# Attention in a Trainium2 decoder layer: keys and values in a phase of their own through DRAM, units of four heads by 256 rows

## The reference, cut to what matters

```
k = (K @ Wk.T + bk).reshape(n, lk, H, D)      # K = V = ctx, (32, 77, 256); H 16, D 64
v = (V @ Wv.T + bv).reshape(n, lk, H, D)
scores = jnp.einsum('nqhd,nkhd->nqkh', q, k) / jnp.sqrt(jnp.float32(D))
attn = jax.nn.softmax(scores, axis=2)
out = jnp.einsum('nqkh,nkhd->nqhd', attn, v)
out = out.reshape(n, lq, H * D)
return (out @ Wo.T + bo).reshape(n, lq, E)
```

## Time and profile before

| | us |
|---|---|
| median of 3 runs | 2664.46 |
| lowest and highest | 2661.05, 2668.21 |
| profiled execution | 2667.21 |
| its span, first to last instruction | 2665.4 |
| TensorE busy | 2418.4 (91%) |
| VectorE busy | 1942.1 (73%) |
| ScalarE busy | 1349.4 (51%) |
| GpSimd busy | 1274.9 (48%) |

### The profile page before, as it was taken

One profiled execution on the slowest core, in us unless ns is written; L12 is line 12 of the kernel. 1 busy time (PEld: TensorE's weight loads), 2 busy tenths in 40 slices (PEclk: granted clock), 3 DMA queues, 4 the chain that ended last, 5 costly groups with the idle time before them and its releaser, 6 DMA issues. The chain is left out here.

```text
span 2665.4 us, 60791 instructions
## 1 busy us (share of the span) xinstructions
PE 2418.4 (91%) x18124; PEld 2197.3 (82%) x18125; DVE 1942.1 (73%) x5342; ACT 1349.4 (51%) x2881; POOL 1274.9 (48%) x1444
## 2 busy tenths in 40 slices
PE   7999999999968999999999999999992999999866
PEld 5777777777757999999999999999992899999833
DVE  7988888888854666666666666666672778877768
ACT  5555565655544544444444444444441566665523
POOL 4676667676642222233222332223321677876656
PEclk9999999999979999999999999999996999999955
DMA  3011111111011111211111111111107677776578
GB/s 133 29 36 35 31 30 32 35 35 35 28 38 63 56 49 55 67 66 53 57 54 66 66 48 63 54 66 66 45 33 287 227 242 252 246 253 221 185 246 272
DMA packets 170802, 263.44 MB, mean 99 GB/s; under 512 B 33560, under 2 KB 123296, under 8 KB 170720
## 3 DMA queue, kind: packets, MB, share of 16 engines
q1 hardware_dynamic: 156672, 225.70, 26.1%
q0 software_dynamic: 12960, 35.67, 3.7%
q10 hardware_dynamic: 1088, 1.07, 0.1%
HBM read 180.79 MB, written 81.59 MB: 98 GB/s over the span
## 5 line engine op out<-in xcount | busy, mean ns | idle before, releaser
L1290 ACT ACTIVATE b_qT<-b_ps_qk,b_bq_c 128x256 f32<-128x256 f32 x256 | 121.6, 475 | 397.8 <-PE b_ps_qk L1134 397.8
L1371 DVE TENSOR_REDUCE b_mx<-b_ps_s 128x4 f32<-128x308 f32 x256 | 121.6, 475 | 204.9 <-PE b_ps_s L1167 110.1
L1189 PE MATMUL b_ps_o<-b_vv,b_pT 77*128 77x65 f32 x2048 | 259.5, 269 | 0.8 <-DVE b_o_n L1391 0.8
L1189 PEld LDWEIGHTS b_ps_o<-b_vv,b_pT 77*128 77x128 f32 x2048 | 248.7, 192 | 6.2 <-issue 5.4
L570 DVE SCALAR_TENSOR_TENSOR a_conv<-a_xc_pad,a_cw,a_conv 128x256 f32<-128x256 f32 x384 | 236.1, 674 | 9.4 <-ACT a_conv L457 9.4
L1301 ACT ACTIVATE b_pe_<-b_sd 128x308 f32<-128x308 f32 x256 | 118.0, 461 | 217.9 <-DVE b_sd L1375 215.1
L1589 POOL TENSOR_TENSOR b_ve<-b_mv,b_ln_eps 128x1 f32<-128x1 f32 x64 | 12.2, 191 | 412.9 <-DVE b_mv L1414 412.9
L1977 POOL DMA_INDIRECT made_scratch<-c_o_s,c_to x142 | 150.2, 1058 | 90.7 <-issue 48.5
L112 PE MATMUL c_ps_h<-c_xT_hi,c_w 128*128 128x256 f32 x568 | 169.0, 298 | 23.6 <-DMA c_b_c<-in_c_b 14.6
L1167 PE MATMUL b_ps_s<-b_kz,b_qT 128*128 128x154 f32 x1024 | 188.3, 306 | 0.0
L112 PE MATMUL c_ps_o<-c_w,c_h_hi 128*128 x568 | 161.4, 284 | 20.1 <-DMA c_w<-parts_scratch 16.5
(11 more groups left out here) (266 smaller groups left out, 8563.7 us busy)
## 6 DMA issues: line engine op xcount, KB each, us to landing
c_w<-parts_scratch SPq DMA_DIRECT2D x79, 1024.0 KB, 16.3
c_xa<-sent_scratch SPq DMA_DIRECT2D x71, 260.0 KB, 2.7
parts_scratch<-b_w_cut SPq DMA_DIRECT2D x32, 512.0 KB, 4.6
d_got<-made_scratch SPq DMA_DIRECT2D x32, 512.0 KB, 5.4
a_xT_f<-in_xT SPq DMA_DIRECT2D x32, 256.0 KB, 3.1
a_x_f<-in_x SPq DMA_DIRECT2D x32, 256.0 KB, 2.6
x_scratch<-a_x_t SPq DMA_DIRECT2D x32, 256.0 KB, 2.2
b_xa<-x_scratch SPq DMA_DIRECT2D x32, 256.0 KB, 2.9
```

The source lines that it names most:

```text
L1189: last = pe.matmul(ps_o[:, (HD + 1) * i:(HD + 1) * i + HD + 1], pT[:, u.par, i, :], vv[:, b.par, G * g + i, :], start=True, stop=True)
L1290: act.activation(qT[:, b.par, m, :], ps_qk[:, 0:L], ACT.Identity, bias=bq_c[:, m:m + 1])
L1371: dve.tensor_reduce(mx[:, u.par, :], s, AX.X, ALU.max).then_inc(s_mx, 1)
```

## The change

The keys and the values of all sequences are computed ahead of the attention, in `keys_values_phase`, with float32r splits for both. It works on chunks of eight sequences: two groups of four sequences (308 wide) for the keys and five tiles of up to 128 context rows for the values, and writes both to DRAM (10.1 MB each). The cutting of the experts' 32 weight parts moves here too, with its loads (8.4 MB) and stores (16.8 MB). The working space lies in what will be `w2`.

In the attention a unit is four heads by all 256 rows, so a step has four turns. Keys and values come back from DRAM. The negated maximum is the bias of the exponential, which makes one instruction per 77 columns: eight in a unit. VectorE sums the exponentials and divides them before they are turned. `attend` has the values stationary, 64 columns for one head, and the turned probabilities moving, 256 wide; the even head of a pair goes to partitions 0 to 63 of the result and the odd one to 64 to 127. The result is already turned, so `turn_o` is gone. `ps_s`, which was two banks used in turn, is now one pair of banks that the next unit waits for. The experts' `w2` and rows are loaded in the attention's first eight steps (`load_later`).

```diff
-    PER = 8
+    PER = 4
...
+            def load_part(i):
+                if i >= 2:
+                    sp.wait_ge(s_cut_lo, i - 1)
+                sp.dma_start(w_raw[:, i % 2, :], routing.w_parts[i, :, :]).then_inc(s_raw[i % 2], 16)
+
+            def store_part(i):
+                sp.wait_ge(s_cut_lo, i + 1)
+                sp.dma_start(routing.parts[i, :, :],
+                             w_cut[:, i % 2, :, :].rearrange("p h n -> p (h n)").bitcast(F32)).then_inc(s_cut_out[i % 2], 16)
...
+            def store_keys(i):
+                sp.wait_ge(s_kc, MH * (i + 1))
+                sp.dma_start(keys[GROUP * i:GROUP * i + GROUP, :, :].rearrange("s p n -> p s n"),
+                             k_s[:, i % 2, :, :, :].rearrange("p s m k -> p s (m k)")).then_inc(s_k_out[i % 2], 16)
...
+            def store_values(ch, t):
+                i, (r, n) = ch * len(TILES) + t, TILES[t]
+                sp.wait_ge(s_vc, 2 * (i + 1))
+                sp.dma_start(values[ROWS * ch + r:ROWS * ch + r + n, :], v_s[0:n, i % 2, :]).then_inc(s_v_out[i % 2], 16)
...
+            for ch in range(CHUNKS):
+                for sub in range(SUBS):
+                    next_part()
+                    next_part()
+                    store_keys(ch * SUBS + sub)
+                if ch + 2 < CHUNKS:
+                    load_c(ch + 2)
+                for t in range(len(TILES)):
+                    next_part()
+                    store_values(ch, t)
...
+                for sub in range(SUBS):
+                    for m in range(MH):
...
+                        for k in range(KD):
+                            last = split3(pe, ps_k[i % 4][:, 0:N],
+                                          (wk_hi[:, k, P * m:P * m + P], wk_lo[:, k, P * m:P * m + P]),
+                                          (c_hi[:, par, k, N * sub:N * sub + N], c_lo[:, par, k, N * sub:N * sub + N]),
+                                          k == 0, k == KD - 1)
+                        last.then_inc(s_k, 1)
...
+                        for k in range(KD):
+                            last = split3(pe, ps_v[i % 4][0:n, :], (c_hi[:, par, k, r:r + n], c_lo[:, par, k, r:r + n]),
+                                          (wv_hi[:, k, 512 * half:512 * half + 512],
+                                           wv_lo[:, k, 512 * half:512 * half + 512]), k == 0, k == KD - 1)
+                        last.then_inc(s_v, 1)
...
+                    for m in range(MH):
+                        act.wait_ge(s_k, i * MH + m + 1)
+                        act.activation(k_s[:, i % 2, :, m, :], ps_k[(i * MH + m) % 4][:, 0:N].rearrange(
+                            "p (s k) -> p s k", s=GROUP), ACT.Identity, bias=weights.bk_c[:, m:m + 1]).then_inc(s_kc, 1)
...
+            for i in range(PARTS):
+                pool.wait_ge(s_raw[i % 2], 16 * (i // 2 + 1))
+                if i >= 2:
+                    pool.wait_ge(s_cut_out[i % 2], 16 * (i // 2))
+                pool.tensor_copy(w_cut[:, i % 2, 0, :], w_raw[:, i % 2, :]).then_inc(s_cut_hi, 1)
+                pool.wait_ge(s_cut_hi, i + 1)
+                pool.tensor_tensor(w_cut[:, i % 2, 1, :], w_raw[:, i % 2, :], w_cut[:, i % 2, 0, :].bitcast(F32),
+                                   ALU.subtract).then_inc(s_cut_lo, 1)
...
-        ps_s = [ctx.enter_context(nc.psum_tensor(f"b_ps_s{i}", [P, 512], F32)) for i in range(2)]
...
+        ps_s = ctx.enter_context(nc.psum_tensor("b_ps_s", [P, GM, 512], F32))
...
+            def load_keys(b):
+                if not b.before(2):
+                    sp.wait_ge(s_s, b.ago(2).count(4, 4))
+                for a in range(2):
+                    half = slice(HD * a, HD * a + HD)
+                    sp.dma_start(kz[half, b.par, a, :, :].rearrange("p m k -> p (m k)"),
+                                 keys[bass.ds(b.value(), 1), half, :].rearrange("o p n -> (o p) n")
+                                 ).then_inc(s_kz_in[b.par], 16)
+
+            def load_values(b):
+                if not b.before(2):
+                    sp.wait_ge(s_oT, b.ago(2).count(4, 4))
+                sp.dma_start(vv[:, b.par, :], values[bass.ds(b.value() * LK, LK), :]).then_inc(s_vv_in[b.par], 16)
...
+            def load_later(b):
+
+                if b.known() and b.value() < E:
+                    e = b.value()
+                    sp.dma_start(w2[:, e, :, :, :].rearrange("p q h n -> p q (h n)").bitcast(F32),
+                                 routing.parts[4 * e + 2:4 * e + 4, :, :].rearrange("q p n -> p q n")).then_inc(s_ahead, 16)
+                    sp.dma_start(weights.rows[:, e, :, :], rows_in[e, 0:2, :].partition_broadcast(P)).then_inc(s_ahead, 16)
...
-                for k in range(KD):
-                    split3(pe, ps_qk[:, 0:L], (wq_hi[:, k, P * m:P * m + P], wq_lo[:, k, P * m:P * m + P]),
-                           (xT_hi[:, b.par, k, :], xT_lo[:, b.par, k, :]), k == 0, k == KD - 1)
-                for k in range(KD):
-                    last = pe.matmul(ps_qk[:, L:L + LK], wk_f[:, k, P * m:P * m + P], c_f[:, b.par, k, :],
-                                     start=(k == 0), stop=(k == KD - 1))
-                last.then_inc(s_qk, 1)
...
+                    pe.wait_ge(s_qc, u.ago(1).count(1, 1))
+                for i in range(GM):
+                    at = slice(P * (GM * g + i), P * (GM * g + i) + P)
                     for k in range(KD):
-                        last = split3(pe, ps_x[0:LK, :], (c_hi[:, b.par, k, :], c_lo[:, b.par, k, :]),
-                                      (wv_hi[:, k, 512 * half:512 * half + 512],
-                                       wv_lo[:, k, 512 * half:512 * half + 512]), k == 0, k == KD - 1)
-                    last.then_inc(s_v, 1)
-                return run
+                        last = split3(pe, ps_q[:, L * i:L * i + L], (wq_hi[:, k, at], wq_lo[:, k, at]),
+                                      (xT_hi[:, b.par, k, :], xT_lo[:, b.par, k, :]), k == 0, k == KD - 1)
+                last.then_inc(s_q, 1)
...
+                pe.wait_ge(s_qc, u.count(1, 1))
+                if not u.before(1):
+                    pe.wait_ge(s_exp, u.ago(1).count(1, 1))
                 for i in range(GM):
-                    last = pe.matmul(ps_s[u.par][:, 2 * LK * i:2 * LK * i + 2 * LK],
-                                     qT[:, b.par, GM * g + i, P * j:P * j + P],
-                                     kz[:, b.par, GM * g + i, :, :].rearrange("p a k -> p (a k)"),
-                                     start=True, stop=True)
+                    for j in range(NT):
+                        last = pe.matmul(s_scores[:, i, 2 * j:2 * j + 2, :], qT[:, u.par, i, P * j:P * j + P],
+                                         kz[:, b.par, :, GM * g + i, :], start=True, stop=True)
...
+                for i in range(GM):
+                    for j in range(NT):
+                        for a in range(2):
+                            at = L * a + P * j
+                            last = pe.transpose(ps_pT[0:LK, i, at:at + P], pn[:, u.par, 4 * i + 2 * j + a, :], ident)
                 last.then_inc(s_pT, 1)
...
-                for i in range(G):
-                    last = pe.matmul(ps_o[:, (HD + 1) * i:(HD + 1) * i + HD + 1], pT[:, u.par, i, :],
-                                     vv[:, b.par, G * g + i, :], start=True, stop=True)
-                last.then_inc(s_o, 1)
...
                 for i in range(GM):
-                    last = pe.transpose(ps_oT[:, P * i:P * i + P], flat[:, P * i:P * i + P], ident)
+                    for a in range(2):
+                        at = HD * (G * g + 2 * i + a)
+                        last = pe.matmul(ps_oT[HD * a:HD * a + HD, L * i:L * i + L], vv[:, b.par, at:at + HD],
+                                         pT[:, u.par, i, L * a:L * a + L], start=True, stop=True)
                 last.then_inc(s_oT, 1)
...
+            def turn_x2(b):
+                pe.wait_ge(s_x2, b.count(NT, NT))
+                if over(b, 3):
+                    pe.wait_ge(s_base, b.ago(1).count(1, 1))
+                else:
+                    pe.wait_ge(s_xlo, b.ago(-3).count(1, 1))
+                if not b.before(1):
+                    pe.wait_ge(s_x2c, b.ago(1).count(1, 1))
+                for j in range(NT):
...
             run_steps(pe, n_seq, by_unit(
-                [(queries_keys, 0, 1), (scores, 0, 2), (turn_p, 1, 2), (attend, 2, 2), (turn_o, 3, 2), (project, 4, 2)],
-                {0: [(values(0), 1)], 1: [(turn_x2(0), 3)], 2: [(rank, 4)], 3: [(values(1), 1)], 4: [(gate(0), 3)],
-                 5: [(turn_x, 0)], 6: [(turn_x2(1), 3)], 7: [(gate(1), 3)]}), peel=8)
+                [(queries, 0, 1), (scores, 1, 1), (turn_p, 3, 1), (attend, 4, 1), (project, 5, 1)], {},
+                {0: [(rank, 4)], 1: [(turn_x, 0)], 2: [(turn_x2, 3)], 3: [(gate, 3)]}), peel=8)
...
+                for c in range(C):
+                    last = act.activation(pe_[:, u.par, c, :], s_scores[:, c // (C // GM), c % (C // GM), :], ACT.Exp,
```

(58 more changed lines are left out.)

631 lines of the change are left out of this document (292 added, 339 removed).

## The result

| | before | after |
|---|---|---|
| median of 4 runs, us | 2666.34 | 2473.47 |
| lowest and highest | 2661.05, 2670.03 | 2468.74, 2481.10 |
| profiled execution's span | 2665.4 | 2473.7 |
| TensorE busy | 2418.4 | 2201.1 |
| mean granted clock | 0.953 | 0.944 |

The changed kernel takes 0.928 of the time before (95% interval 0.925 to 0.931), 193 us less. The forecast was 2516, the range 2451 to 2635.

The account below looks back on a forecast made before the run. TensorE was taken to bound the attention. Against the profiled 2667.2 us, -297 for the attention, +168 for the new phase, -5 and -17 for small terms sum to -151, so 2516 us; range 2451 to 2635.

Parts of the forecast that it names:

- the sum: Whole kernel: attention -297, new phase +168, way to the first query -5, w2 loads -17, together -151 us.
- eight take the time of five: Attend: eight half-width records overlap only between neighbours on different halves, 1.19 us, taken as 1.3 with changes of width.
- the bound of fully abreast: Attend's lower bound: two heads of a pair run fully side by side on different column halves, 0.95 us.
- the change of width: Attend: going to half width and back on TensorE costs about 0.1 us a unit, 13 us in all.
- the rival of the drain: Attend: changing to half width and back empties TensorE, 41 us in place of 13, 2544 us; chance 0.08.
- The new phase: Keys and values ahead of the attention: SyncE's queue sets it, +168 us, bounds 148 and 185.
- the sum over rounds: New phase: SyncE's rounds of load, cut and store make 124.5 us for three chunks and 34 for the last.
- The rival of the slow clock: New phase: TensorE falls to 1.2 GHz, +53 us, 2569 us; chance 0.07.
- The small ones: Attention's start loses the cuts of Wq and Wo, -5 us; experts lose the wait for w2, -17 us.
- The cover over ScalarE: Attention: ScalarE's chain round the loop takes 6.65 us against a turn of 6.97, 0.3 of cover.
- The slower rival: Attention: ScalarE's chain sets the turn; exponentials at 0.50 and attend at 2.0 give 2757 us; chance 0.04 for slower.
- The wait in turn 2: Attention: turning x2 waits for the low part of the next x, 0.8 us a step including handing over.

Follow-up runs that it names:

- number 1: Changed kernel with attend at whole width, 128 columns of values stationary and a pair's two matmuls adding up: 2552.9 us.
- number 3: Changed kernel with attend writing both heads of a pair to the same column half from the second unit on: 2582.3 us.
- number 4: Changed kernel with turning and attend issued in halves by pair, four changes of width a unit in place of two: 2526.3 us.
- number 2: Changed kernel with attend running the heads on columns 0 to 63 first, then those on columns 64 to 127: 2469.1 us.
- numbers 5: Changed kernel with four buffers for the weight parts in place of two, each part stored three rounds after its load: 2454.2 us.
- number 6: Changed kernel with only the first two weight parts cut and stored, and used by all experts: 2444.2 us.
- number 9: Changed kernel with the loads of w2 and of the rows back at the start of the experts: 2494.9 us.
- number 11: Changed kernel with 16 exponentials a unit on ScalarE in place of 8, the extra ones into spare room: 2586.4 us.

## Why the prediction was right, point by point

**The attention** gave 342 where the sum had 297. It was right that TensorE alone sets the step: it is busy 590.31 of 600, and what is added to its row is paid in full (numbers 1, 3 and 4). Of the 45 that the sum missed, a turn 0.28 shorter makes 36, the rest of the step 6, and filling and draining 2. Two terms were mis-sized. First, the step "records in strict order can overlap only where neighbours lie on different halves, so eight take the time of five" failed: they take the time of four, whatever the order (number 2), and the bound of fully abreast was the true one. Second, the change of width, taken at 0.1 a unit: in the trace it is 0.09 before attend (a transpose leads on in 0.11, but attend starts 0.20 behind the last one), 0.05 at its first pair and 0.10 before the projection, 0.25 in all; number 4 measured 0.30 for two changes. Against number 1 it comes to 0.33, since from the last record of attend to the second of the projection it is 0.53 here and 0.34 at whole width. Attend and its changes together are 1.10 where 1.3 stood: 26 us of the 45. The Trainium skill, TensorEngine Tiling (Array Packing), section Key Properties, has both: changing the mode drains TensorE, and tiles load and multiply in parallel. The runs agree with the second (number 3). With the first they agree in price, 0.15 a change in number 4, near the 0.16 that the unhidden part of a record gave; that TensorE stands empty at a change is not shown, as the first half-width record starts 0.20 behind a transpose that the profile, whose ends of matmuls are modelled, gives 0.27. The second outweighs the first here: by number 1 whole width, with no changes, costs 72 more in the attention. So the rival of the drain was near the truth in its price (41 said, 0.25 to 0.33 x 128 = 32 to 42 measured), and its 2544 failed because attend itself was cheaper. The other terms: scores 1.05 for 1.14, turning 0.97 with its 0.09 for 0.86, the rest of a step 2.3 for 2.5. The turn came to 6.06 for 6.34.

**The new phase** was put at 168 and took 172 by SyncE's first load to the attention's (792.7 to 964.9). The mechanism is shown by numbers 5 and 6: the round of load, cut and store over two buffers set it, the bandwidth would have come 28 us lower and TensorE 45 lower. That the whole came within 4 us is in part luck, as three errors offset each other. The first three chunks lasted 37.0, 44.7 and 38.0, together 119.7 for the 124.5 in the sum, the last 37.1 for 34, and the two ends together 15 for 9.6; the sum over rounds was right for the whole and not chunk by chunk. The rival of the slow clock saw a real thing, 0.79 to 0.87 granted in three chunks, but its price was not paid: TensorE still waited 31.9 us for free staging between 833 and 957, and without the waits the clock was full (number 6).

**The small ones.** The way from the attention's first load to its first query is 6.4 (964.9 to 971.3), 6 was said. The stretch behind the last projection lost 17.2, and number 9 brought 21 back; as the experts differed by up to 20 between the profiled executions of this study, the 17 is confirmed as a wait (14.9 in the trace) and not as a sum to the microsecond.

**The cover over ScalarE** was called thin, 0.3. It was 0.4 to 1.6, turn by turn. The exponentials with a bias start 0.21 apart in a row, eight in 1.82 or 0.23 apiece, and not 0.315. No row of before had shown the 0.21 that the prediction put at its low end:

```profile
1403.08 1.02 ACT L1468 ACTIVATE b_pT<-b_ps_pT 77x1024 f32<-77x1024 f32 x1 [1.08 <-PE b_ps_pT L1366]
1404.10 0.60 ACT L1474 ACTIVATE b_oT_hi<-b_ps_oT 128x512 fp32r<-128x512 f32 x1
1404.59 1.82 ACT L1460 ACTIVATE b_wk_f<-b_ps_s,b_nmx 128x77 f32<-128x77 f32 x8
```

And the chain doesn't run over attend, as I had it: the high part starts when ScalarE's own copy of the turned exponentials ends (1404.10), some 0.1 behind attend. Corrected, it is 1.05 + 0.97 + 1.02 + 0.6 + 1.82 + 0.2 = 5.66, and with 3.66 of exponentials 7.5, which number 11 hit with 7.42. The slower rival needed exponentials of 0.5: number 11, at an equal load of 0.46, is still 80 us faster than before.

**The wait in turn 2** was put at 0.8 and is 0.42; its removal gave 0.63 a step.

In all: the attention 45 better than said, the phase with the way to the first query 4 worse, the stretch behind within 1, so the forecast was 42 too high.

## What to carry to other kernels

Two matmuls of half width on different column halves ran at the price of one here, in both orders that were tried, but each change of width cost about 0.15 us: put all half-width work of a unit together, and count what is saved per group (0.86 us here) against one pair of changes (0.30). Work that is moved out of a full stage into one of its own is paid in full, and there the order of one DMA queue over two buffers can cost more than bytes or matmuls, as it did here; look for a stage with an idle queue and an idle engine first, as the attention was for the weight parts. Before calling a cover thin, follow the chain through each engine's own list, since an engine can be busy with something else than the link that was assumed.

## What was unexpected of the hardware

Two half-width records that stand four apart in the program start together (0.44 for the pair in number 2), so each column half takes its work ahead of the other's. A change of width costs 0.15 (number 4). ScalarE's exponentials of 77 columns with a bias from SBUF start 0.21 apart in a row, though each is 0.347 long on the mean; their starts are what counts, as with matmuls.
